# A graph-attention edge stage on one core: record columns made three groups in advance, sums ahead of the logits' transpose, PSUM banks in turn across groups

## The reference

```python
feat_all = einsum('ni,rhid->rnhd', layernorm(x), conv_weights)   # 8 relations, 4 heads, 64 wide
el = sum(feat_all[type, src] * attn_l[type], -1)
er = sum(feat_all[type, dst] * attn_r[type], -1)
e  = leaky_relu(el + er, 0.2)
m  = segment_max(e, dst);   ex = exp(e - m[dst])
alpha = ex / segment_sum(ex, dst)[dst]
h = segment_sum(alpha[..., None] * feat_all[type, src], dst) + h_bias
x = x + h          # then: x + top-2 of 8 experts(layernorm(x))
```

## Time and profile before

| | us |
|---|---|
| median of 3 runs | 2532.44 (2530.4 to 2534.8) |
| the profiled execution's own time | 2529.42 |
| its span in the profile | 2527.6 |
| TensorE busy in the span | 1860.7 (74%) |
| VectorE busy | 1148.7 (45%) |
| GpSimd busy | 1078.7 (43%) |
| ScalarE busy | 819.7 (32%) |

### The profile page before, as it was taken

One profiled execution on the slowest core, in us unless ns is written; L12 is line 12 of the kernel. 1 busy time (PEld: TensorE's weight loads), 2 busy tenths in 40 slices (PEclk: granted clock), 3 DMA queues, 4 the chain that ended last, 5 costly groups with the idle time before them and its releaser, 6 DMA issues. The chain is left out here.

```text
span 2527.6 us, 38608 instructions
## 1 busy us (share of the span) xinstructions
PE 1860.7 (74%) x9120; PEld 1578.4 (62%) x9121; DVE 1148.7 (45%) x2882; ACT 819.7 (32%) x2109; POOL 1078.7 (43%) x1151
## 2 busy tenths in 40 slices
PE   6799377777777777877777878754119999999920
PEld 6688366666566665666666666544118888888820
DVE  2132136666566666666666667668411111111122
ACT  1122154444435344444444444301003223222200
POOL 1000077777676767676677777500440000000046
PEclk9899758887888788888888888875559999999965
DMA  5633244444333433343344344210135655555533
GB/s 192 249 135 153 83 117 112 111 113 107 93 106 103 109 99 106 103 111 103 102 108 106 104 113 110 77 49 17 56 138 177 205 179 201 190 193 200 184 91 113
DMA packets 127778, 317.14 MB, mean 125 GB/s; under 512 B 27207, under 2 KB 78151, under 8 KB 114020
## 3 DMA queue, kind: packets, MB, share of 16 engines
q0 software_dynamic: 53568, 148.39, 21.8%
q1 hardware_dynamic: 74020, 166.61, 19.1%
HBM read 251.75 MB, written 63.14 MB: 125 GB/s over the span
## 5 line engine op out<-in xcount | busy, mean ns | idle before, releaser
L552 POOL DMA_INDIRECT gath<-feats,idxT x996 | 947.1, 951 | 683.8 <-DVE ndlT L583 339.3
L840 PE MATMUL psP<-gath,hot 128*128 128x260 f32 x1992 | 627.6, 465 | 97.5 <-DVE acc L676 94.6
L840 PEld LDWEIGHTS psP<-gath,hot 128*128 128x128 f32 x1992 | 429.9, 229 | 194.3 <-DVE acc L676 108.6
L762 ACT ACTIVATE hot<-cst,ndlT 128x128 f32<-128x128 f32 x996 | 317.1, 392 | 46.7 <-DVE ndlT L583 31.5
L772 ACT COPY hotT<-psOT 128x512 f32<-128x512 f32 x249 | 144.3, 580 | 570.3 <-PE psOT L811 569.9
L667 DVE TENSOR_TENSOR gath<-gath,psA 128x1024 f32<-128x1024 f32 x249 | 301.2, 1220 | 18.0 <-ACT gath L789 11.3
L825 PEld LDWEIGHTS psE<-er,hotT 128*128 128x128 f32 x1992 | 280.7, 216 | 33.7 <-issue 31.4
L825 PE MATMUL psE<-er,hotT 128*128 x1992 | 278.5, 287 | 23.2 <-issue 23.2
L676 DVE TENSOR_TENSOR acc<-acc,psP 128x260 f32 x498 | 210.2, 422 | 116.7 <-PE psP L840 75.7
L1224 PE MATMUL psH<-xeT,w1buf 128*128 128x256 f32 x1184 | 262.8, 380 | 0.0
L1235 PE MATMUL psY<-w2buf,hT 128*128 128x256 f32 x1184 | 261.5, 379 | 0.0
(11 more groups left out here) (190 smaller groups left out, 1220.3 us busy)
## 6 DMA issues: line engine op xcount, KB each, us to landing
w1buf<-in_experts SPq DMA_DIRECT2D x37, 1030.0 KB, 7.2
w2buf<-in_experts SPq DMA_DIRECT2D x37, 1024.0 KB, 5.4
feats<-frow SPq DMA_DIRECT2D x30, 1040.0 KB, 3.9
gath<-feats,idxT POOLq DMA_INDIRECT x996
slots_x<-acc SPq DMA_DIRECT2D x1, 9472.0 KB, 32.1
xrow<-slots_x SPq DMA_DIRECT2D x37, 256.0 KB, 6.5
slots_y<-yrow SPq DMA_DIRECT2D x37, 256.0 KB, 6.6
meta<-in_edges SPq DMA_DIRECT2D x512, 12.0 KB
```

The costliest lines, as they stand in the source:

```text
L552: pool.indirect_dma_start(gath[:, r, u], None, feats, bass.IndirectOffsetOnAxis(ap=idxT[:, q, u:u + 1], axis=0)).then_inc(gath_in[r], 16)
L762: ins = act.activation(hot[:, q, u], iota, ACT.Square, bias=ndlT[:, q, u:u + 1])
L840: ins = pe.matmul(psP[:, b % BANKS, 0:FW], hot[:, q, u], gath[:, r, u], start=u % BLK == 0, stop=u % BLK == BLK - 1)
```

## The change

Three edits in `edge_stage`:

1. The records' columns are made in period g for group g + 3, not g + 2. The tiles `reset`, `cat`, `idxT`, `ndlT` and `typeT` get three places (by r) for two (by q). Ahead of period 0 stand groups 0, 1 and 2, not 0 and 1, on VectorE and on TensorE. `meta` keeps two places.
2. In slot 0 TensorE's sums of quad 3 of the group before stand ahead of the logits' transpose, not behind it.
3. The banks of `psP` go in turn over all pairs of all groups, so that every pair waits for the third pair before it and no more.

```diff
+        def bank(g, b, r):
+            return ((BASES[g] if isinstance(g, int) else GB * r) + b) % BANKS
...
-                meta_rows(0, 0)
-                meta_columns(0, 0)
-                meta_rows(1, 1)
-                meta_columns(1, 1)
+                for g in range(GBUFS):
+                    meta_rows(g, g % 2, g)
+                    meta_columns(g, g)
                 pick_right(0, 0)
...
-                    if there(g + 2):
-                        meta_rows(g + 2, q)
+                    if there(g + 3):
+                        meta_rows(g + 3, 1 - q, r)
...
-                        if b >= BANKS:
-                            pe.wait_ge(sum_used, pairs_before(g) + b - BANKS + 1)
-                        elif not isinstance(g, int) or g > 0:
-                            pe.wait_ge(sum_used, pairs_before(g))
+                        if not isinstance(g, int) or pairs_before(g) + b >= BANKS:
+                            pe.wait_ge(sum_used, pairs_before(g) + (b - BANKS + 1))
                         for u in range(b * BLK, (b + 1) * BLK):
-                            ins = pe.matmul(psP[:, b % BANKS, 0:FW], hot[:, q, u], gath[:, r, u],
+                            ins = pe.matmul(psP[:, bank(g, b, r), 0:FW], hot[:, q, u], gath[:, r, u],
...
-                meta_rows(0)
-                meta_rows(1)
+                for g in range(GBUFS):
+                    meta_rows(g)
                 for j in range(SLOTS_Q):
                     turn(0, 0, j)
...
                         turn(g + 1, 1 - q, s)
-                        if s == 0:
-                            pe.wait_ge(e_ready, g + 1)
-                            pe.transpose(psS[:, S_ET:S_ET + P], e_sb[:, 1], ident).then_inc(eT_ready, 1)
                         right_logits(g + 1, s - 1)
-                        if s == 5 and there(g + 2):
-                            meta_rows(g + 2)
+                        if s == 5 and there(g + 3):
+                            meta_rows(g + 3)
...
                     slot(0)
+                    pe.wait_ge(e_ready, g + 1)
+                    pe.transpose(psS[:, S_ET:S_ET + P], e_sb[:, 1], ident).then_inc(eT_ready, 1)
                     slot(1)
```

More of the change, by code:

```diff
@@ L559, in _, with meta_rows @@
                 step = Chain(dve, v_step)
-                def meta_rows(g, q):
+                def meta_rows(g, q, r):
                     dve.wait_ge(meta_in[q], 8 * GB * g + 16 * GB - 8 * GB * q)
@@ L668, in scale, with add @@
                                       ALU.mult).then_inc(scaled, 1)
-                def add(g, j, into):
+                def add(g, j, r, into):
                     if j >= quads(g):
@@ L675, in add @@
                         dve.wait_ge(sum_ready, pairs_before(g) + b + 1)
-                        dve.tensor_tensor(into[b % PQ], into[b % PQ], psP[:, b % BANKS, 0:FW], ALU.add).then_inc(sum_used, 1)
+                        dve.tensor_tensor(into[b % PQ], into[b % PQ], psP[:, bank(g, b, r), 0:FW], ALU.add).then_inc(sum_used, 1)
                         dve.wait_ge(sum_used, pairs_before(g) + b + 1)
@@ L704, in period @@
                     logits(g, r, n)
-                    add(before, 2, sums2)
+                    add(before, 2, rb, sums2)
                     scale(before, rb, 4)
-                    chunk_maxima(g, q)
-                    add(before, 3, sums3)
+                    chunk_maxima(g, r)
+                    add(before, 3, rb, sums3)
                     scale(before, rb, 5)
@@ L713, in period @@
                     chain_maxima(g, q)
-                    add(before, 4, sums4)
+                    add(before, 4, rb, sums4)
                     scale(before, rb, 6)
@@ L717, in period @@
                     sums5, sums6 = load_tiles(before, 5), load_tiles(before, 6)
-                    shifts(g, q)
-                    add(before, 5, sums5)
-                    add(before, 6, sums6)
+                    shifts(g, r)
+                    add(before, 5, rb, sums5)
+                    add(before, 6, rb, sums6)
                     dve.wait_ge(exp_ready, g + 1)
@@ L731, in period @@
                     sums1 = load_tiles(g, 1)
-                    if there(g + 2):
-                        meta_columns(g + 2, q)
-                    add(g, 0, sums0)
+                    if there(g + 3):
+                        meta_columns(g + 3, r)
+                    add(g, 0, r, sums0)
                     scale(g, r, 2)
-                    add(g, 1, sums1)
+                    add(g, 1, r, sums1)
                     scale(g, r, 3)
                     if there(g + 1):
-                        pick_right(g + 1, 1 - q)
+                        pick_right(g + 1, (r + 1) % GBUFS)
                     assert isinstance(g, int) or step.n == STEPS, step.n
@@ L747, in _, with one_hot @@
                     scale(last, r, j + 2)
-                    add(last, j, load_tiles(last, j))
+                    add(last, j, r, load_tiles(last, j))
             @block.scalar
             def _(act):
-                def one_hot(g, q, j):
+                def one_hot(g, q, r, j):
                     if j >= quads(g):
@@ L761, in one_hot @@
                         u = j * QUAD + k
-                        ins = act.activation(hot[:, q, u], iota, ACT.Square, bias=ndlT[:, q, u:u + 1])
+                        ins = act.activation(hot[:, q, u], iota, ACT.Square, bias=ndlT[:, r, u:u + 1])
                     ins.then_inc(squared, 1)
@@ L772, in copy, with both @@
                     act.copy(hotT[:, j % 2], psOT[:]).then_inc(hotT_copied, 1)
-                def both(g, q, js):
+                def both(g, q, r, js):
                     for j in js:
-                        one_hot(g, q, j)
+                        one_hot(g, q, r, j)
                         if j:
                             copy(g, j - 1)
-                both(0, 0, range(SLOTS_Q))
+                both(0, 0, 0, range(SLOTS_Q))
                 copy(0, SLOTS_Q - 1)
                 def period(g, q, r, n):
-                    both(g + 1, 1 - q, range(5))
+                    both(g + 1, 1 - q, (r + 1) % GBUFS, range(5))
                     act.wait_ge(dnT_ready, g + 1)
@@ L790, in period @@
                                    ACT.Exp).then_inc(exp_ready, 1)
-                    both(g + 1, 1 - q, range(5, SLOTS_Q))
+                    both(g + 1, 1 - q, (r + 1) % GBUFS, range(5, SLOTS_Q))
                     copy(g + 1, SLOTS_Q - 1)
```

48 lines of the change are left out of this document (24 added, 24 removed).

## The result

The changed kernel takes 2545.09 us (median of 9 runs, 2540.41 to 2557.41) where the kernel before takes 2530.88 (9 runs): a ratio of 1.0065, interval 1.0044 to 1.0086. It is slower by 14 us, 0.65%; 9.5 us faster was forecast. On a second chip of the kind (experiment d1) it was 2558.85 against 2530.13, 1.0095 [1.0074, 1.0115].

A forecast was written before the change was run, and what follows sets the result against it. A ring between TensorE and VectorE was taken as the bound. Gains of 24.0 (loop), 3.5 (written out) and 2.0 us (groups 29, 30), less 20.0 at the start, gave 9.5 us faster, 2522.9 us; range 2500 to 2544.

The forecast's parts named there:

- GpSimd off the path: Edge stage periods: gathered data lie ready over 12 us early, so removing GpSimd's 3.9 us wait a period gains nothing.
- The start, 20.0 us: Ahead of period 0: waiting for group 2's records delays group 0's logits, a loss of 20.0 us, once.
- Banks in turn, 0.3 us a period: Pair 0's wait goes: 0.3 us a period gained in the loop, 1 us each for groups 29 and 30.
- Sums ahead of the transpose, 0.5 us a period: Slot 0: pair 6 runs inside TensorE's wait, gaining 0.5 us a period, bounds -0.3 and 0.9.
- Clock, +0.2 us a period: Odd loop periods: less idle removes some half-clock stretches at two pairs, gaining 0.2 us a period, ends 0 and 0.8.
- Rival B: Slot 0: VectorE does not win back the late transpose; 12.2 us slower, 2544.6 us; chance 0.23.
- my rival of 0.02: Cycling PSUM banks each iteration makes TensorE swing between clocks, one more half-clock stretch a period; 29 us slower; chance 0.02.

The follow-up runs named there:

- d2: Kernel before with GpSimd's 32 indirect gathers a group replaced by 8 plain transfers of as many bytes (plain loads): 2528.81 us, 0.9986 of before.
- h1: Changed kernel with real gathers, group 2's start rows and columns behind group 0's right logits, pair 6 summed four times: 2486.36 us, 0.9828 of before.
- h2: Kernel before plus banks in turn, pair 6 summed four times ahead of the logits' transpose, pair 7 behind it, no advance: 2487.21 us, 0.9832 of before.
- f1: Kernel before with plain loads and banks in turn alone: 2518.52 us, 0.9945 of before.
- f2: Kernel before with plain loads, sums ahead of the transpose and banks in turn, no advance: 2539.00 us, 1.0033 of before.
- d4: Kernel before with plain loads and the second edit alone, both pairs' sums ahead of the logits' transpose: 2568.65 us.
- d3: Changed kernel, all three edits, with plain loads in place of the gathers: 2546.69 us.
- f4: Kernel before with plain loads, banks in turn, pair 6's sum ahead of the logits' transpose and pair 7's behind it: 2535.05 us, 1.0002 of before.
- f3: Changed kernel with plain loads, pair 6 summed four times into the same bank to keep TensorE busy in the wait: 2506.53 us, 0.9900 of before.
- c2: Second edit alone, sums ahead of the transpose, on a chip where the kernel before takes 3690.24 us: 3702.03 us, 1.0030 of before.

## Why the prediction was wrong

- **GpSimd off the path:** right. d2 shows it without any gathers, and h1 and h2 show it with them.
- **The start, 20.0 us:** right in mechanism and size, 20.4 at group 0 and 18.6 at group 1; h1 takes it back.
- **Banks in turn, 0.3 us a period:** right in total (10.3 us over 31 periods, f1 against d2), in part by luck: that is the sum of pair 0's wait, which is gone wherever the edit is in, of the half clock that went with it (1.5 to 0.0 us a period), and of six more late periods. But edits do not add: beside the sums ahead it is worth 29.7 us (f2 against d4), where half clock falls from 19.5 to 15.3 us a period, the stretch at pair 0 above all.
- **Sums ahead of the transpose, 0.5 us a period:** this step failed, in sign. "I take 0.5 us a period, near the end where the half clock lasts" let the half clock last through `turn` and `right_logits`. In 11 of 24 periods it lasts through slot 1 as well, which moves L621 to t + 10.2 where the forecast's worst was a loss of 0.3. In the two real kernels L621 starts 8.62 us behind the logits on average where it was 8.25: 0.4 us lost a period ahead of it, where 0.5 were to be gained. f2 against f1 measures the whole term: -0.66 us a period by the medians. The bound was worked out from where the half clock ended in the kernel before; but the edit takes a pair out of the very burst that used to lie under it, and behind nearly equal idle times the clock came back within slot 0 or only behind slot 1. That the pair taken out is what makes periods late is my reading of three comparisons (late periods 2 to 13 from d2 to d3, 8 to 11 from f1 to f2, 8 to 21 from f1 to f4). It is not all of it: from d2 to f1 they go from 2 to 8, and slot 0 is the same there. What decides between the two kinds is open.
- **Clock, +0.2 us a period:** right as far as it went. The term priced the stretch at pairs 0 and 1, and the half clock from 28 to 34 us behind the logits fell from 1.6 us a period to 0.0. With the banks' term it made more than the 0.5 forecast: the period is 0.3 us shorter although 0.4 were lost ahead of L621, so 0.7 were won behind it. What the term left out was the clock of slot 1. The pair taken ahead cuts the idle time from 5.66 to 5.2 us and does not close it.

By the account of the loop, 7.6 us were gained where 24 were forecast, 1.0 of 5.5 in the part written out, and 18.6 of 20.0 were lost; 2.1 more were lost behind group 31's logits, for which I have no cause. Rival B had the result (2544.6), and the point from which it decides: 0.65 us a period were needed, under 0.3 came. It had also named the half clock that holds through `turn` and `right_logits`, though not that it could hold through slot 1. That its sum met the median within 0.5 us is luck: its main mechanism, a late transpose not won back, is only part. VectorE does wait 0.57 us more, but f4 has no late transpose and loses to f1.

The Trainium skill (TensorE: Matmul & The Clock Gate, "HAM oscillation") says that idle gaps between bursts return the array to half rate. The runs agree: behind about 5 us of idle the burst starts at 0.50 in the changed kernel, and only 1 of 72 periods is late in f3, h1 and h2, where mostly 2 to 3 us are left. I had used it to argue that the burst starts at half rate with or without the edit, and that the sum is the same. The first half held; how far into the program the half rate reached was what changed. The Trainium skill's section "A second HAM failure mode: psum-queue depth-cycling", my rival of 0.02, did not come about: letting the banks run on took half clock away at pair 0 (2.6 to 0.0 us a period from d4 to f2), and no kernel became slower by it.

The advance seems to gain in the loop: d3 is 7.7 us above f2, and the start alone should make it 20. Most of that is where a pass of the loop ends. VectorE's logits at the first such place, in f2 and in d3:

```profile
649.08 0.29 DVE L600 TENSOR_TENSOR e_sb<-gath,er_e 128x128 f32<-128x128 f32 x1 [8.58 <-issue]
```

```profile
669.82 0.29 DVE L600 TENSOR_TENSOR e_sb<-gath,er_e 128x128 f32<-128x128 f32 x1 [5.94 <-issue]
```

Elsewhere this wait is 3.0 us on average. Over the three places between groups 1 and 25 it adds up to 25.7 to 26.8 us in the five kernels with plain loads and no advance (d2, d4, f1, f2, f4), and to 18.0 to 19.5 in all others, with gathers or with the advance. So d3 has 7.8 us less of it than f2: it comes from the plain loads without the advance, not from the change in the real kernel (19.1 us, before 18.7). Why is open. Without it d3 would stand some 26 us above d2 by my estimate (17.9 and the 8.4 between their sums), and on that chip the real kernels are 28.7 us apart (d1). The rest may be the clock's scatter: d3's profile is of its slowest run, f2's of its fastest.

## What to carry to other kernels

Price a move of matmuls by the clock that it leaves behind, not by their own durations: here taking work out of the burst behind an idle time cost more than the work taken out. Ask at which place of the chain the half clock lies, not how much of it there is. Where TensorE must wait about 5 us in each period, try to fill the wait, even with work thrown away, and check in the trace that it is filled; here 12 spare matmuls in a period gave 40 us. And a loader's advance belongs behind the first group's critical work, not ahead of it.

## What the runs showed of the hardware

- Very little goes with a stretch of half clock: a wait of 0.19 us at pair 0, behind other small gaps, and two pairs take 3.07 us instead of 1.92. No kernel with banks in turn had that stretch on these chips.
- The same program, in neighbouring periods and behind nearly the same idle time (5.21 and 5.17 us), gets the full clock back either within slot 0 or not before the end of slot 1, and the changed kernel's nine runs differ by 0.7%, the slower ones at a lower mean clock (0.822 to 0.823 against 0.828 to 0.831).
- On two chips this kernel took 3685 and 3690 us instead of 2531. In c2 TensorE stood still for 30 to 46 us in each of 24 periods; in the one shown this began while GpSimd issued its 32 gathers and ended 12 us behind them. The rank order of the edits is another one there.
- At the end of a pass of the loop VectorE stands about 6 us ahead of its next instruction where it otherwise stands 3.0, and 8.4 to 9.2 us in the kernels with plain loads and no advance.
